# Turning the expert mask on VectorE in 32-column blocks, in an audio tower kernel of one core

## The chip, the cores and the metric

The kernel runs on one core of one Trainium2 chip. The metric is device time in microseconds (us) of one execution, from several executions; the profile comes from one further execution, whose own time is given beside its span.

Engines are named as in the profile: PE is TensorE's matmul stream, PEld its weight loads (LDWEIGHTS), DVE is VectorE, ACT is ScalarE, POOL is GpSimd, SP is SyncE, whose queue issues the DMAs here.

## What is computed

```python
# x: [16, 375, 256] float32; row 0 of each batch entry is the readout row
h = gelu(x[:, 1:] @ W_other + x[:, :1] @ W_read + b)     # [16, 374, 256]
h = h + cosine_attention(layernorm(h))                   # softmax of cosines, + its input
h = h + moe_attention(layernorm(h))
# moe_attention, per token t and expert e (8 experts, D = 128):
logits = (x/|x|) @ (sim/|sim|) - sigmoid(gates)
mask   = (relu(logits) > 0), or the two largest where no expert is active
r      = softmax over the active experts of relu(logits)
q, k, v = sum_e mask[t, e] * (x[t] @ W_{q,k,v}[e])       # each [T, 128]
a      = softmax(causal(q k^T / sqrt(128))) v
out    = sum_e mask*r[t, e] * (a[t] @ W_o[e])
```

So for every batch entry a 0/1 mask of 374 tokens by 8 experts is worked out, and the normalised rows x are multiplied by it, once for every expert, before the q, k and v products.

## The kernel before, in words

Tokens lie in NT = 3 tiles of 128 (TP = 384, the last tile holds 118), channels in NC = 2 chunks of 128, E = 8. Every float32 product is made as three fp16 products of high and low parts (split_product, from L1616; its three matmuls carry L1620). The 16 batch entries run through a software pipeline. One step works on up to four entries at once: `g1` (first layer norm), `f` (cosine attention, second layer norm, router, mask), `m` (the q, k, v products, called "units" M(0) to M(23), six matmuls each) and `n` (scores, softmax, and the output products, called "pairs" 0 to 11, three matmuls of 512 columns each). The pipeline (from L325) has an early step, one step with fixed indices, a hardware loop of 12 steps, one more full step with fixed indices, and two shorter ones. The 12 + 2 full steps have both an `f` and an `n`. Ahead of the pipeline a head embeds all entries and takes the first ones through their first stages.

Each engine has its order of work written out by hand, and engines meet only through semaphores. What matters around the change, in a full step:

- PE (its `step`, second half) runs M(12), logits(f), pair 2, M(13), M(14), pair 3, M(15), turn_mask(f), pair 4, M(16), pair 5 and so on. logits gives the router's products. turn_mask (L1701 to L1706) transposes the three tiles of mask16, each 128x128 of which 8 columns are used, into a PSUM bank. pair(n, p) waits until DVE has added pair p-2 (s_pair_added), since two PSUM banks alternate: pair 4 needs the additions of pairs 0, 1 and 2.
- DVE runs pairs(0, 2), route(f), pairs(2, 4), weight_max, head_low of k, pairs(4, 5) and so on. route (L1168 to L1213) is the chain of small operations that goes from the router's products to the mask; nearly all of them wait for the one before. Its last two write the mask, once as mask16 in fp16 (L1211) and once as lg[8] in float32 (L1212) for POOL. add_pair (L1130 to L1137) is the addition of one pair from PSUM to h.
- ACT copies the turned mask to maskT, 8x384 (turned_mask, L798 to L802), between the scaling of pairs 3 and 4, and then evacuates k (head_high).
- SP, in mask_around (L423 to L433), waits for maskT, stores it to DRAM in one DMA (8 rows of 768 B), waits for that, and loads it back, spread over 128 partitions, in two DMAs of half the experts each. mask_tokens (from L1215) on DVE multiplies x by it, one expert at a time; the first one is called after pair 8 has been added.

Of the kernel before, what the change touches and what calls it, by code (L numbers as in the profile page):

```python
# [26 lines left out]
def audio_tower_kernel(nc, x, tok_w, tok_b, sim_matrix, gates, q_proj, k_proj, v_proj, o_proj, out):  # L27
# [6 lines left out]
    NC = C // P  # L34
    PAIRS = NT * E // 2

    KEYS = [min((i + 1) * P, T) for i in range(NT)]
# [7 lines left out]
    with ExitStack() as ctx:  # L45
# [3 lines left out]
        def sem(name):  # L49
            return ctx.enter_context(nc.semaphore(name))  # L50
# [50 lines left out]
        row3 = sb("row3", [P, 6, NT])  # L101
        mask16 = sb("mask16", [P, NT, P], F16)
        maskT = sb("maskT", [E, TP], F16)
        mask_all = sb("mask_all", [P, E, TP], F16)
        route_w = sb("route_w", [P, B, NT, E])
        xm = sb("xm", [P, E, 2 * NC, TP], F16)
# [53 lines left out]
        d_route = nc.dram_tensor("d_route", [(NT - 1) * E * P], F32, kind="Internal").ap()  # L160
        d_mask = nc.dram_tensor("d_mask", [B, E * TP], F16, kind="Internal").ap()

# [95 lines left out]
        s_route_exp = sem("route_exp")  # L258
        s_mask_turned = sem("mask_turned")
        s_mask_row = sem("mask_row")  # L260
# [114 lines left out]
        def _(sp):  # L375
# [47 lines left out]
            def mask_around(f):  # L423

                sp.wait_ge(s_mask_row, f + 1).then_inc(s_sp_passed, 1)
                sp.dma_start(d_mask[f, :].rearrange("(e t) -> e t", e=E), maskT[:, :]).then_inc(s_mask_stored, 16)
                sp.wait_ge(s_mask_stored, 16 * (f + 1)).then_inc(s_sp_passed, 1)
                if later(f):
                    sp.wait_ge(s_xm_ready, E * f).then_inc(s_sp_passed, 1)
                for k in range(2):  # L430
                    sp.dma_start(mask_all[:, k * (E // 2):(k + 1) * (E // 2), :].rearrange("p e t -> p (e t)"),
                                 d_mask[f, k * (E // 2) * TP:(k + 1) * (E // 2) * TP].partition_broadcast(P)).then_inc(
                                     s_mask_loaded[k], 16)  # L433
# [266 lines left out]
        def _(act):  # L700
# [8 lines left out]
            act.wait_ge(s_pad_zeroed, 1)  # L709
            a.activation(unused[:, :], mask16[:, 0, 0:1], ACT.Gelu)  # L710

# [85 lines left out]

            def turned_mask(f):  # L798
                act.wait_ge(s_mask_turned, f + 1)
                if later(f):  # L800
                    act.wait_ge(s_mask_stored, 16 * f)
                a.activation(maskT[:, :], as16(turn[1] if later(f) else turn[0], TP)[0:E, :], ACT.Copy).then_inc(s_mask_row, 1)  # L802

            def route_exp(f):
# [47 lines left out]
            def step(i, g1, f, m, n):  # L852
# [20 lines left out]
                if early(m):  # L873
                    weights_high(2 * NC - 1)
                    turned_rows_2(f)
                    weights_high(2 * NC)
                    weights_high(2 * NC + 1)
                    head_high(qT, qkv_bank[0], s_q_done, m + 1, s_q_hi, [], qkv_out)
                    turned_mask(f)
                    route_exp(f)  # L880
                    head_high(kT, qkv_bank[1], s_k_done, m + 1, s_k_hi, [], qkv_out)
                    high(0, g1)
                    output_weights_high(0)
                    output_weights_high(1)
                    turned_rows(g1)
                    high_v()
                    return
# [28 lines left out]
                if f is not None and n is not None:  # L916
                    scale_pairs(0, 4)
                    turned_mask(f)
                    head_high(kT, qkv_bank[1], s_k_done, m + 1, s_k_hi, [(s_scores_done, NT * m)], qkv_out)
                    scale_pairs(4, 5)  # L920
                    route_exp(f)
                    scale_pairs(5, 7)
                    if g1 is not None:
                        high(0, g1)
                    scale_pairs(7, PAIRS)
                    if g1 is not None:
                        turned_rows(g1)
                    high_v()
                    return
# [66 lines left out]
            exp_cosines(1, (2,))  # L996
            turned_mask(0)
            route_exp(0)
# [10 lines left out]
        def _(dve):  # L1009
            v = nc.vector  # L1010


            v.memset(mask16[:, 0, :], 0.0).then_inc(s_pad_zeroed, 1)
            v.memset(h[96:P, 0:1, NT - 1, :], 0.0).then_inc(s_zeroed, 1)
# [5 lines left out]
            v.memset(read_hl[:, :], 0.0).then_inc(s_zeroed, 1)  # L1020
            v.memset(mask16[:, 1:NT, :], 0.0)

# [145 lines left out]
            def route(b):  # L1168
# [20 lines left out]
                if later(b):  # L1189
# [17 lines left out]
                                             row3[:, 1, :].unsqueeze(2).broadcast_to([P, NT, E]),  # L1207
                                             ALU.is_lt, ALU.mult))
                if later(b):
                    dve.wait_ge(s_mask_turned, b)  # L1210
                v.tensor_tensor(mask16[:, :, 0:E], lg[:, 0, :, :], M, ALU.add).then_inc(s_mask_ready, 1)  # L1211
                v.tensor_tensor(lg[:, 8, :, :], lg[:, 0, :, :], M, ALU.add).then_inc(s_mask_ready, 1)  # L1212
                assert at[0] == RP  # L1213
# [302 lines left out]
        def _(pe):  # L1516
# [43 lines left out]
            for k in range(WARM):  # L1560
                t_.matmul(bank[6][:, 0:P], mask16[:, 0, :], mask16[:, 0, :], start=True, stop=True)  # L1561
            pe.wait_ge(s_consts, 1)
# [6 lines left out]
            for k in range(FILL):  # L1569
                t_.matmul(bank[6][:, 0:P], mask16[:, 0, :], mask16[:, 0, :], start=True, stop=True)  # L1570
            pe.wait_ge(s_tok_read, 16)
# [26 lines left out]
            def turn_first_high(b):  # L1598

                pe.wait_ge(s_hi1, b + 1)  # L1600
                if not isinstance(b, int) or b > 1:
                    pe.wait_ge(s_logits_out, b)
                    pe.wait_ge(s_mask_row, b)
                turn_rows(0, b, 0, turn[0], s_turned1_hi)
# [83 lines left out]
            def logits(f):  # L1688
# [10 lines left out]
                last.then_inc(s_logits_done, 1)  # L1699

            def turn_mask(f):  # L1701
                pe.wait_ge(s_mask_ready, 2 * (f + 1))
                pe.wait_ge(s_T2_lo, f + 1)
                for t in range(NT):
                    last = t_.transpose(as16(turn[1] if later(f) else turn[0], TP)[:, t * P:(t + 1) * P], mask16[:, t, :], ident16[:, :])  # L1705
                last.then_inc(s_mask_turned, 1)  # L1706

# [95 lines left out]
            def step(i, g1, f, m, n):  # L1803
# [19 lines left out]
                if early(m):  # L1823
# [5 lines left out]
                    M(*range(7, 13))  # L1829
                    turn_mask(f)  # L1830
                    M(*range(13, 22))
# [6 lines left out]
                if f is not None and n is not None:  # L1838
# [37 lines left out]
                    M(15)  # L1876
                    turn_mask(f)
                    pair(n, 4)
# [13 lines left out]
                pe.wait_ge(s_logits_out, B)  # L1892
                pe.wait_ge(s_mask_row, B)
                turn_v(n)
# [74 lines left out]
            turn_in(13)  # L1969
            turn_mask(0)  # L1970
            dots(1, 2)
# [9 lines left out]
            pe.wait_ge(s_hi2, 2)  # L1981
            pe.wait_ge(s_mask_row, 1)
            turn_rows(1, 1, 0, turn[0], s_turned2_hi)
# [26 lines left out]
```

## Time and profile before

| | |
|---|---|
| median of 3 runs | 712.61 us (712.33 to 713.15) |
| the profiled execution's own time | 712.67 us |
| its span, first to last instruction | 710.9 us |
| granted TensorE clock | 1.00 of full speed |
| busy: PE / PEld | 705.6 us (99%) / 472.8 us (66%) |
| busy: DVE / ACT / POOL | 579.4 us (81%) / 378.8 us (53%) / 400.5 us (56%) |
| one loop step | 40.50 us |

In a row of a timeline the columns are start in us from the span's start, duration in us, engine, line, operation, output and input tiles with shapes, the count of instructions merged into the row, and in brackets the idle time before it and what ended it. PE matmuls are pipelined and overlap, so that the start of the next group, not the duration of this one, tells what a group cost. A line inside a helper stands for all its callers; the tile names tell them apart: `xm,w_qkv` are the units M, `w_o,aoT` the pairs, `ident,mask` the turned mask.

### The profile page before, as it was taken

To read this page: it belongs to the slowest core of one execution; us is meant where nothing else is said; L and a number is where in the kernel's file an instruction comes from. 1 tells how busy PE (TensorE), PEld (TensorE's weight loads), DVE (VectorE), ACT (ScalarE), POOL (GpSimd) and SP (SyncE) were. 2 spreads that over 40 slices of the span, in tenths; PEclk is the share of its full clock that TensorE was granted. 3 is DMA by queue.
4 is the path that set the end of the run, shared out by engine and by line. 5 is a ranking of instruction groups with operands and counts; after the bars stand their busy time and mean duration, and the time that the engine had idled before them with its cause. 6 is when DMAs were issued, how large, how long until landed. Compare 5 with 4: busy or idle time off the path is not lost.

```text
span 710.9 us, 18143 instructions
## 1 busy us (share of the span) xinstructions
PE 705.6 (99%) x5416; PEld 472.8 (66%) x5416; DVE 579.4 (81%) x1453; ACT 378.8 (53%) x808; POOL 400.5 (56%) x655
## 2 busy tenths in 40 slices
PE   9999999999999999999999999999999999999997
PEld 8888666675757666575756666575766667575655
DVE  5788798888879888888979888887988888886636
ACT  4977373554646464563646355463646455464443
POOL 7652325757465566746566575746566674643434
DMA  9671210202020010202020010202011020201120
GB/s 246 159 179 46 75 43 13 67 3 65 12 63 14 25 52 0 70 7 63 14 56 22 12 66 0 70 7 63 14 34 43 0 70 7 63 17 53 16 74 30
DMA packets 33430, 34.35 MB, mean 48 GB/s; under 512 B 7288, under 2 KB 29176, under 8 KB 33272
## 3 DMA queue, kind: packets, MB, share of 16 engines
q1 hardware_dynamic: 33152, 33.78, 17.7%
q8 instruction: 16, 0.26, 0.2%
q10 hardware_dynamic: 248, 0.19, 0.1%
q14 instruction: 14, 0.11, 0.1%
HBM read 27.70 MB, written 6.26 MB: 48 GB/s over the span
## 4 chain that ended last, share of the span: by engine, by line
PE 98%; DVE 1%; ACT 0%; issue 0%; DVEq 0%
PE bank L1620 76%; PE bank L1683 7%; PE bank L1537 4%; PE bank L1594 3%; PE bank L1526 2%; PE bank L1754 1%; PE bank L1669 1%; PE bank L1542 1%; PE bank L1732 1%; PE bank L1561 1%; PE bank L1705 0%; PE bank L1694 0%; PE bank L1697 0%; ACT xm L836 0%; PE bank L1795 0%
## 5 line engine op out<-in xcount | busy, mean ns | idle before, releaser
L1620 PE MATMUL bank<-xm,w_qkv 128*128 128x374 f16 x2304 | 415.7, 322 | 0.0
L1620 PEld LDWEIGHTS bank<-xm,w_qkv 128*128 128x128 f16 x2304 | 220.8, 98 | 139.2
L866 ACT ACTIVATE region_c<-bank,out_w 128x256 f32<-128x256 f32 x180 | 84.6, 470 | 163.5 <-PE bank L1620 162.5
L1224 DVE TENSOR_TENSOR xm<-xT,mask_all 128x1496 f16<-128x1496 f16 x128 | 151.8, 1208 | 0.0
L1620 PE MATMUL bank<-w_o,aoT 128*128 128x512 f16 x540 | 143.3, 379 | 0.0
L1136 DVE SCALAR_TENSOR_TENSOR h<-bank,out_w,h 128x256 f32 (+1 forms) x180 | 86.5, 480 | 49.1 <-ACT region_c L866 44.3
L645 POOL TENSOR_TENSOR region_c<-region_c 128x512 f32<-128x512 f32 x46 | 76.4, 1661 | 27.8 <-ACT region_c L866 23.1
L660 POOL TENSOR_TENSOR exp_hl<-exp,exp_hl 128x128 f16<-128x128 f32 (+2 forms) x48 | 41.9, 873 | 83.8 <-ACT exp_hl L822 83.3
L1620 PEld LDWEIGHTS bank<-w_o,aoT 128*128 128x128 f16 x540 | 50.5, 98 | 39.6
L1115 DVE TENSOR_SCALAR region_b<-h,moments,small 128x256 f32 (+1 forms) x96 | 48.8, 552 | 6.1 <-POOL small L566 6.1
L648 POOL TENSOR_TENSOR region_c<-region_c 128x256 f32<-128x256 f32 x46 | 47.9, 1041 | 8.2 <-POOL region_c L645 8.2
L1683 PE MATMUL bank<-xhl,exp_hl 128*128 128x257 f16 (+1 forms) x432 | 50.3, 272 | 0.0
L651 POOL TENSOR_TENSOR h<-region_c,h 128x256 f32 (+1 forms) x46 | 38.0, 827 | 15.8 <-POOL region_c L648 11.4
L1683 PEld LDWEIGHTS bank<-xhl,exp_hl 128*128 128x128 f16 x432 | 41.6, 97 | 7.3
L745 ACT ACTIVATE xhl<-region_b 128x768 f16<-128x768 f32 x32 | 27.0, 844 | 33.1 <-DVE region_b L1115 33.1
L775 ACT ACTIVATE region_a<-region_a,log_p,small 128x374 f32<-128x374 f32 (+2 forms) x48 | 28.2, 587 | 26.4 <-DVE region_a L1235 26.4
L562 POOL TENSOR_SCALAR small<-moments 128x3 f32<-128x3 f32 x32 | 14.4, 449 | 49.4 <-DVE moments L1107 49.4
L1620 PE MATMUL bank<-xT 128*128 128x374 f16 (+2 forms) x288 | 37.8, 268 | 0.0
L1537 PE MATMUL bank<-w_tok,xinT 128*128 128x256 f16 x288 | 37.6, 273 | 0.0
L850 ACT ACTIVATE pT<-bank 128x768 f16<-128x768 f16 x16 | 13.0, 810 | 46.0 <-PE bank L1754 46.0
L1098 DVE BATCH_NORM_STATS2 stats<-h 128x6 f32 (+1 forms) x96 | 35.7, 413 | 0.0
L576 POOL TENSOR_TENSOR small<-small,m_half 128x3 f32<-128x3 f32 x32 | 28.3, 884 | 8.1 <-POOL small L572 8.1
(198 smaller groups left out, 1064.4 us busy)
## 6 DMA issues: line engine op xcount, KB each, us to landing
mask_all<-d_mask SPq DMA_DIRECT2D x32, 384.0 KB, 3.8
h<-in_x_dram SPq DMA_DIRECT2D x16, 256.0 KB, 4.9
out_dram<-h SPq DMA_DIRECT2D x32, 128.0 KB
rnorm_row<-d_rnorm SPq DMA_DIRECT2D x16, 192.0 KB, 3.8
out_dram<-h SPq DMA_DIRECT2D x16, 112.0 KB
h<-in_x_dram SPq DMA_DIRECT2D x15, 112.0 KB, 5.2
xm<-in_L_ffn_q_proj_dram SPq DMA_DIRECT2D x2, 512.0 KB, 7.6
region_c<-in_L_ffn_k_proj_dram SPq DMA_DIRECT2D x2, 512.0 KB, 6.2
```

Source lines behind the costliest of these rows:

```text
L645: g.tensor_tensor(prod_sum[:, 0:2, :], prod[:, buf, 0:2, :], prod[:, buf, 2:4, :], ALU.add).then_inc(s_tile_summed, 1)
L648: g.tensor_tensor(prod_sum[:, 2, :], prod_sum[:, 0, :], prod_sum[:, 1, :], ALU.add).then_inc(s_tile_summed, 1)
L651: g.tensor_tensor(h[:, n, t, :], prod_sum[:, 2, :], h[:, n, t, :], ALU.add).then_inc(s_tile_ready, 1)
L660: done = g.tensor_tensor(exp2_hl[:, 1, sl], exp2[:, sl], exp2_hl[:, 0, sl], ALU.subtract)
L866: a.activation(prod[:, prod_buf(n, t), q, :], pair_bank(n, p)[:, C:2 * C], ACT.Copy, scale=weights_out(n)[:, t, 2 * q + 1:2 * q + 2]).then ...
L1098: v.bn_stats(stats[n][:, t, :], h[:, b, t, :]).then_inc((s_stats1, s_stats2)[n], 1)
L1115: v.tensor_scalar(xs[n][:, t, :], h[:, b, t, :], moments[n][:, t, 0:1], small[n][:, 4, t:t + 1], ALU.subtract, ALU.mult).then_inc((s_xs1, ...
L1136: v.scalar_tensor_tensor(h[:, n, t, :], pair_bank(n, p)[:, 0:C], weights_out(n)[:, t, e0:e0 + 1], h[:, n, t, :], ALU.mult, ALU.add).then_i ...
L1224: v.tensor_tensor(xm[:, e, :, 0:T], xT[1][:, :, :, 0:T].rearrange("p a c t -> p (a c) t"), mask_all[:, e, 0:T].unsqueeze(1).broadcast_to([ ...
L1537: t_.matmul(projected(t), xinT[:, b % 2, xp, c, t * P:(t + 1) * P], w_tok[:, wp, c, :], start=(c == 0 and xp == 0 and wp == 0), stop=False ...
L1620: last = t_.matmul(dst, left[lp], right[rp], start=(starts and k == 0), stop=(stops and k == 2), skip_group_check=True)
L1683: last = t_.matmul(banks[t][:, 0:n], exp1_hl[:, ep, j, t * P:(t + 1) * P], xhl[0][:, xp, j, 0:n], start=(j == 0 and k == 0), stop=(j == NT ...
```

## The change

DVE turns the mask itself. mask16 shrinks to 32 columns, with column e*3 + t for expert e and token tile t (24 used). After the two mask operations of route, DVE waits for the first of them, waits for the stores of the previous entry's mask, and transposes the 128x32 tile in four 32x32 blocks into mask_turned: row q*32 + e*3 + t holds the mask of tokens 32q to 32q+31 of tile t. SP stores the four blocks in four DMAs of 24 rows of 64 B, such that DRAM holds what it held before (expert, then token), and loads it back as before. PE's three transposes, their two waits, the waits of PE and DVE for their result and ACT's copy are gone. The block of zeros that warms PE up is now a part of mask_all.

```diff
+    SQ = 32
...
-        mask16 = sb("mask16", [P, NT, P], F16)
-        maskT = sb("maskT", [E, TP], F16)
+        mask16 = sb("mask16", [P, SQ], F16)
+        mask_turned = sb("mask_turned", [P, SQ], F16)
...
                 sp.wait_ge(s_mask_row, f + 1).then_inc(s_sp_passed, 1)
-                sp.dma_start(d_mask[f, :].rearrange("(e t) -> e t", e=E), maskT[:, :]).then_inc(s_mask_stored, 16)
-                sp.wait_ge(s_mask_stored, 16 * (f + 1)).then_inc(s_sp_passed, 1)
+                rows = d_mask[f, :].rearrange("(r b j) -> b r j", r=SQ, j=SQ)
+                for q in range(P // SQ):
+                    sp.dma_start(rows[q][0:NT * E, :], mask_turned[q * SQ:q * SQ + NT * E, :]).then_inc(s_mask_stored, 16)
+                sp.wait_ge(s_mask_stored, 16 * (P // SQ) * (f + 1)).then_inc(s_sp_passed, 1)
...
-            def turned_mask(f):
-                act.wait_ge(s_mask_turned, f + 1)
-                if later(f):
-                    act.wait_ge(s_mask_stored, 16 * f)
-                a.activation(maskT[:, :], as16(turn[1] if later(f) else turn[0], TP)[0:E, :], ACT.Copy).then_inc(s_mask_row, 1)
...
                 if later(b):
-                    dve.wait_ge(s_mask_turned, b)
-                v.tensor_tensor(mask16[:, :, 0:E], lg[:, 0, :, :], M, ALU.add).then_inc(s_mask_ready, 1)
-                v.tensor_tensor(lg[:, 8, :, :], lg[:, 0, :, :], M, ALU.add).then_inc(s_mask_ready, 1)
+                v.tensor_tensor(mask16[:, 0:NT * E].rearrange("p (e t) -> p t e", t=NT), lg[:, 0, :, :], M,
+                                ALU.add).then_inc(s_mask_ready, 1)
+                v.tensor_tensor(lg[:, 8, :, :], lg[:, 0, :, :], M, ALU.add).then_inc(s_mask_ready, 1)
+                dve.wait_ge(s_mask_ready, 2 * b + 1)
+                if later(b):
+                    dve.wait_ge(s_mask_stored, 16 * (P // SQ) * b)
+                v.transpose(mask_turned[:, :], mask16[:, :]).then_inc(s_mask_row, 1)
...
-            def turn_mask(f):
-                pe.wait_ge(s_mask_ready, 2 * (f + 1))
-                pe.wait_ge(s_T2_lo, f + 1)
-                for t in range(NT):
-                    last = t_.transpose(as16(turn[1] if later(f) else turn[0], TP)[:, t * P:(t + 1) * P], mask16[:, t, :], ident16[:, :])
-                last.then_inc(s_mask_turned, 1)
```

All calls of turned_mask and turn_mask go too, and PE's waits for s_mask_row in front of later uses of the banks.

## Rows read from the trace of the kernel before

**Rows 1.** The page: busy time and share of the span by engine.
```profile
PE 705.6 (99%) x5416; PEld 472.8 (66%) x5416; DVE 579.4 (81%) x1453; ACT 378.8 (53%) x808; POOL 400.5 (56%) x655
```
**Rows 2.** Busy time by engine in one loop step: start:end, step length, busy us (instructions).
```profile
297.00:337.50 40.50, 40.50 (x310) 26.32 (x308) 34.46 (x88) 21.21 (x47) 24.71 (x40) 1.00 0.12 34
```
**Rows 3.** Waits of PE over the whole span: who for whom, us, times, longest.
```profile
PE bank L1561 <- DVE mask L1013: 1.1, 1, 1.1
PE bank L1620 <- DVE v_tok L1310: 0.4, 1, 0.4
PE bank L1795 <- ACT xm L836: 0.4, 1, 0.4
```
**Rows 4.** Timeline of PE in a loop step, from the router's products to pair 4.
```profile
320.89 0.19 PE L1697 MATMUL bank<-w_sim,xT 128*128 128x8 f16 x2
320.94 0.81 PE L1620 MATMUL bank<-w_o,aoT 128*128 128x512 f16 x3
...
324.13 1.11 PE L1620 MATMUL bank<-xm,w_qkv 128*128 128x374 f16 x6
325.08 0.33 PE L1705 MATMUL bank<-ident,mask 128*128 128x128 f16 x3
325.25 0.38 PE L1620 MATMUL bank<-w_o,aoT 128*128 128x512 f16 x1
```
**Rows 5.** Timeline of PE's weight loads around the turned mask, same step.
```profile
325.08 0.15 PEld L1705 LDWEIGHTS bank<-ident,mask 128*128 128x128 f16 x2
325.19 0.10 PEld L1620 LDWEIGHTS bank<-w_o,aoT 128*128 128x128 f16 x1
```
**Rows 6.** Timeline of DVE in the same step: route and the additions around it.
```profile
321.12 0.21 DVE L1182 COPY logit_parts<-bank 128x48 f32<-128x48 f32 x1
321.36 0.18 DVE L1185 TENSOR_TENSOR lg<-logit_parts 128x24 f32<-128x24 f32 x1
321.57 0.18 DVE L1187 TENSOR_TENSOR lg<-lg,small 128x24 f32<-128x24 f32 x1
321.89 0.18 DVE L1191 TENSOR_TENSOR lg<-lg,sig 128x24 f32<-128x24 f32 x1
...
322.54 0.35 DVE L1196 TENSOR_TENSOR cmp<-lg 128x192 f32<-128x192 f32 x1
322.93 0.18 DVE L1197 TENSOR_REDUCE row<-lg 128x3 f32<-128x24 f32 x1
...
324.47 0.18 DVE L1211 TENSOR_TENSOR mask<-lg 128x24 f16<-128x24 f32 x1
324.57 0.17 DVE L1212 TENSOR_TENSOR lg<-lg 128x24 f32<-128x24 f32 x1
```
**Rows 7.** Timeline of DVE, the addition of pair 2 alone, same step.
```profile
324.67 0.47 DVE L1136 SCALAR_TENSOR_TENSOR h<-bank,out_w,h 128x256 f32 x1
```
**Rows 8.** The same two places in the full step ahead of the loop.
```profile
122.07 1.06 DVE L1136 SCALAR_TENSOR_TENSOR h<-bank,out_w,h 128x256 f32<-128x256 f32 x2
...
122.69 0.10 PEld L1620 LDWEIGHTS bank<-w_o,aoT 128*128 128x128 f16 x1
```
**Rows 9.** Timeline of PEld and PE in the head, where PE waited for DVE.
```profile
58.75 0.11 PEld L1669 LDWEIGHTS bank<-ident,exp_hl 128*128 128x128 f16 x2 [0.24 <-DVE exp_hl L1245]
...
58.76 0.34 PE L1669 MATMUL bank<-ident,exp_hl 128*128 128x128 f16 x3
```
**Rows 10.** Timeline of PE in the head and the early step, around the turned mask.
```profile
55.74 0.33 PE L1705 MATMUL bank<-ident,mask 128*128 128x128 f16 x3
56.02 0.48 PE L1620 MATMUL bank<-xT 128*128 128x118 f16 x6
...
84.41 0.33 PE L1705 MATMUL bank<-ident,mask 128*128 128x128 f16 x3
84.58 0.64 PE L1620 MATMUL bank<-xm,w_qkv 128*128 128x374 f16 x3
```
**Rows 11.** Timeline of ACT, the copy of the turned mask, same loop step.
```profile
325.53 0.48 ACT L802 ACTIVATE maskT<-bank 8x384 f16<-8x384 f16 x1 [0.73 <-PE bank L1705]
325.92 0.45 ACT L751 ACTIVATE kT<-bank 128x374 f16<-128x374 f32 x1
```
**Rows 12.** Timeline of SP's queue in the same step: norms, mask store, mask loads.
```profile
323.79 0.37 SPq L421 DMA_DIRECT2D rnorm_row<-d_rnorm  x1
326.25 0.30 SPq L426 DMA_DIRECT2D d_mask<-maskT  x1
327.93 0.90 SPq L431 DMA_DIRECT2D mask_all<-d_mask  x2
```
**Rows 13.** Timeline of DVE, the first use of the mask in the same step.
```profile
333.58 1.02 DVE L1224 TENSOR_TENSOR xm<-xT,mask_all 128x1496 f16<-128x1496 f16 x1
```
**Rows 14.** DMA issues by line: transfers, count, KB each, median us to landing.
```profile
mask_all<-d_mask SPq DMA_DIRECT2D x32, 384.0 KB, 3.8
...
d_rnorm<-small SPq DMA_DIRECT2D x16, 1.5 KB, 2.4
...
d_route<-route_w SPq DMA_DIRECT2D x1, 8.0 KB, 10.7
```

More of the change, by code:

```diff
@@ L101, in audio_tower_kernel @@
         row3 = sb("row3", [P, 6, NT])
-        mask16 = sb("mask16", [P, NT, P], F16)
-        maskT = sb("maskT", [E, TP], F16)
+        mask16 = sb("mask16", [P, SQ], F16)
+        mask_turned = sb("mask_turned", [P, SQ], F16)
         mask_all = sb("mask_all", [P, E, TP], F16)
+        zeros16 = mask_all[:, 0, 0:P]
         route_w = sb("route_w", [P, B, NT, E])
@@ L160, in audio_tower_kernel @@
         d_route = nc.dram_tensor("d_route", [(NT - 1) * E * P], F32, kind="Internal").ap()
-        d_mask = nc.dram_tensor("d_mask", [B, E * TP], F16, kind="Internal").ap()
+        d_mask = nc.dram_tensor("d_mask", [B, SQ * P], F16, kind="Internal").ap()
         bank = [ctx.enter_context(nc.psum_tensor(f"bank{i}", [P, 512], F32)) for i in range(8)]
@@ L258, in audio_tower_kernel @@
         s_route_exp = sem("route_exp")
-        s_mask_turned = sem("mask_turned")
         s_mask_row = sem("mask_row")
@@ L709, in _ @@
             act.wait_ge(s_pad_zeroed, 1)
-            a.activation(unused[:, :], mask16[:, 0, 0:1], ACT.Gelu)
+            a.activation(unused[:, :], zeros16[:, 0:1], ACT.Gelu)
             def split_in(b):
@@ L878, in step @@
                     head_high(qT, qkv_bank[0], s_q_done, m + 1, s_q_hi, [], qkv_out)
-                    turned_mask(f)
                     route_exp(f)
@@ L917, in step @@
                     scale_pairs(0, 4)
-                    turned_mask(f)
                     head_high(kT, qkv_bank[1], s_k_done, m + 1, s_k_hi, [(s_scores_done, NT * m)], qkv_out)
@@ L996, in _ @@
             exp_cosines(1, (2,))
-            turned_mask(0)
             route_exp(0)
@@ L1010, in _ @@
             v = nc.vector
-            v.memset(mask16[:, 0, :], 0.0).then_inc(s_pad_zeroed, 1)
+            v.memset(zeros16, 0.0).then_inc(s_pad_zeroed, 1)
             v.memset(h[96:P, 0:1, NT - 1, :], 0.0).then_inc(s_zeroed, 1)
@@ L1020, in _ @@
             v.memset(read_hl[:, :], 0.0).then_inc(s_zeroed, 1)
-            v.memset(mask16[:, 1:NT, :], 0.0)
+            v.memset(mask16[:, :], 0.0)
             def token_weights_low():
@@ L1560, in _ @@
             for k in range(WARM):
-                t_.matmul(bank[6][:, 0:P], mask16[:, 0, :], mask16[:, 0, :], start=True, stop=True)
+                t_.matmul(bank[6][:, 0:P], zeros16, zeros16, start=True, stop=True)
             pe.wait_ge(s_consts, 1)
@@ L1569, in _ @@
             for k in range(FILL):
-                t_.matmul(bank[6][:, 0:P], mask16[:, 0, :], mask16[:, 0, :], start=True, stop=True)
+                t_.matmul(bank[6][:, 0:P], zeros16, zeros16, start=True, stop=True)
             pe.wait_ge(s_tok_read, 16)
@@ L1602, in turn_first_high @@
                     pe.wait_ge(s_logits_out, b)
-                    pe.wait_ge(s_mask_row, b)
                 turn_rows(0, b, 0, turn[0], s_turned1_hi)
@@ L1829, in step @@
                     M(*range(7, 13))
-                    turn_mask(f)
                     M(*range(13, 22))
@@ L1876, in step @@
                     M(15)
-                    turn_mask(f)
                     pair(n, 4)
@@ L1892, in step @@
                 pe.wait_ge(s_logits_out, B)
-                pe.wait_ge(s_mask_row, B)
                 turn_v(n)
@@ L1969, in _ @@
             turn_in(13)
-            turn_mask(0)
             dots(1, 2)
@@ L1981, in _ @@
             pe.wait_ge(s_hi2, 2)
-            pe.wait_ge(s_mask_row, 1)
             turn_rows(1, 1, 0, turn[0], s_turned2_hi)
```

## The prediction

> **What bounds the kernel now.** I read the page first: PE is busy 99% of the span, DVE 81% [rows 1]. Then the stretch of one loop step: PE is busy for all of its 40.50 us, DVE for 34.46 [rows 2], and over the whole span PE's waits in the trace add up to 1.9 us [rows 3]. So PE sets the end, and whatever leaves its stream shortens the time, unless something that PE has just not had to wait for comes late instead. A list of waits does not show that second thing: a release that comes in the very last moment leaves no idle time. So the next view is the timeline at the place of the edit, engine by engine.
>
> On PE the three transposes of the mask start at 325.08 and pair 4 starts at 325.25 [rows 4]: they cost 0.17 us. Pair 4's first weight load, which carries pair 4's wait for the addition of pair 2, starts at 325.19 [rows 5]. On DVE that addition stands right behind route; it starts at 324.67 and takes 0.47 us, so it ends at 325.14 [rows 7], 0.05 us before the load that waits for it. Pair 4 is thus at the edge of two chains that both start at the router's products: PE's own (pair 2, M(13), M(14), pair 3, M(15), the transposes) and DVE's (route, whose first copy starts at 321.12, then the addition) [rows 4, 6, 7]. The transposes are the cover under which DVE arrives in time. In the full step ahead of the loop the margin is a little wider: 122.07 + 0.47 = 122.54 against a load at 122.69, 0.15 us [rows 8].
>
> **PE: three transposes removed.** Taken alone 0.17 us a time, 16 times, 2.7 us. In the head it is worth nothing: behind the transposes PE next starts at 56.02 [rows 10], where three transposes at 0.055 us each would have let it start at 55.90, so it waits there for something else. In the early step the next unit starts right behind them, 84.41 to 84.58 [rows 10], with no pair behind it: 0.17 us gained. In the 14 full steps the next instruction is pair 4, and there DVE decides.
>
> **DVE: one transpose and two waits added, between the mask and the addition of pair 2.** Queued behind them are the additions of pairs 2 and 3, weight_max and the low half of k; PE waits for the first of these. Call x the delay of that addition. DVE's rows give what such steps cost, start to start: 0.10 us where the next operation waits for nothing (324.47 to 324.57), 0.21 where it waits for the result just made (321.36 to 321.57), 0.32 where it does so and a second, old semaphore with a value computed from the loop index stands beside it (321.57 to 321.89, L1190) [rows 6]. The last is the form of the new code: the transpose waits for mask16 just written at L1211 and for the old stores with a computed value. The operation on lg[8] lies in the shadow of that wait. So I place the transpose at 324.47 + 0.32 = 324.79.
>
> No row shows a DVE transpose. From below it is a small operation like L1211 that lets the next one start 0.10 us on. From above it is like a 192-element operation which holds the next one for 0.39 (322.54 to 322.93) [rows 6]: it reads 32 elements a partition, far nearer to the 24 of L1211. For the central value I take 0.20, that is 0.10 for the slot and as much again because the addition behind it brings a wait and a computed value of its own, which before lay in the shadow of L1211 and L1212 and now comes behind a stalled queue. The addition then starts at 324.99 instead of 324.67: x = 0.32. The lower bound is 324.47 + 0.21 + 0.10 - 324.67 = 0.11 (second wait and its arithmetic free), the upper 324.47 + 0.32 + 0.39 - 324.67 = 0.51. A gain is excluded here: nothing leaves DVE's chain but a wait for the previous entry's transposes, which is a step old. The strided output of L1211 has as many elements as before; I take it as nothing.
>
> How late is PE then? When PE really waits, its matmul follows the load within 0.01 us (58.75, 58.76) [rows 9]; now it is 0.06 us behind it, 325.19 to 325.25 [rows 4, 5]. So pair 4 can start about 0.05 us closer behind the addition than it does, and a loop step changes by x - 0.05: 0.27 us longer. The 0.17 us that the transposes leave is already in this: the place they leave is filled by waiting. In the two full steps outside the loop (no values to compute, so x about 0.21, margin 0.15) it is 0.06 us longer. Nothing later on PE can win it back, since its stream has no idle time in which to do so [rows 2].
>
> **ACT: the copy removed.** 0.48 us at 325.53, and k is evacuated right behind it [rows 11]. ACT is idle before it and PE's next need of k is a step away: worth nothing, but k comes some tenths earlier, and that is the slack in which the delayed additions of pair 3 and 4 fit.
>
> **SP: four stores in place of one.** Queued behind them are only the loads of the mask and, later, stores of the result; the norms have gone out at 323.79 [rows 12]. The store now starts at 326.25 and the loads at 327.93, 1.68 later. After, SP is released by DVE at about 324.79 + 0.2 = 325.0 and issues at about 325.2. Two issues with their index arithmetic take 0.90, of which one is about 0.37, so each further one is 0.53: the fourth goes out at 326.8. With 1.68 for its way the loads go out at 328.5, and with the 2.4 that a store of 128 short rows takes (d_rnorm) at 329.2 [rows 12, 14]. The first load lands 3.8 us later, at 332.3 to 333.0, and DVE asks for it at 333.58 [rows 13, 14]. Hidden; without that cover DVE's additions of pairs 9 to 11 would wait for it.
>
> As to the short rows: here 1.5 KB in short rows take 2.4 us and 8 KB in single values 10.7 us [rows 14]. The Trainium skill ("DMA: Bandwidth & Descriptors", Specifications) says that line rate needs transfers of at least 512 B and that below it the DMA engine reads, modifies and writes; the rows now stored have 64 B instead of 768 B. By that rule the stores get slower, but for 6 KB the rows above leave it inside the cover.
>
> **The sum**, on the profiled execution's 712.67 us (span 710.9, 1.8 us around it; it lies 0.06 above the median): 12 x 0.27 = 3.2; 2 x 0.06 = 0.1; early step -0.17; head, ACT and SP 0. Together +3.1, so 715.8 us.
>
> **Rivals.**
> First, faster: PE's stream alone decides. It would be so if DVE's additions were hidden, x at most 0.05 (or, to gain anything, below it), the point from which the sign turns. Then 15 x 0.17 = 2.5 us go and the time is 710.1. For it speaks the 99% of PE [rows 1]; against it, that pair 4's load starts 0.05 us behind the addition in this step and that even the cheapest row makes x 0.11. A whole gain needs x below -0.12 in the loop.
>
> Second, the waits cost nothing and only a slot of 0.10 to 0.11 us is added: 12 x (0.11 - 0.05) = 0.7, 2 x (0.11 - 0.15) = -0.1, early -0.17: +0.4, 713.1 us, which a measurement of this kernel can hardly tell from no change (that limit is 0.2%, 1.4 us; 711.2 to 714.0). For it: the two waits are for things that are done or nearly so. Against it: 0.21 and 0.32 between dependent operations [rows 6]. The Trainium skill ("VectorE: DVE Perf Modes", "The DRAIN you can't avoid") says that the next operation starts only when the pipe is empty and that a semaphore costs nothing extra, so that one should count operations, not waits. The rows differ on both: the next operation starts 0.10 us into one of 0.18, and the dependent one 0.21 behind. By that rule one more operation of 0.18 would be all: x = 0.18, +1.6 us from the loop and about 714.1.
>
> Third, the stores land late. It decides from the point where the last of them takes over about 1.7 + 1.3 us. At d_route's 10.7 us the loads would go out at 337.5 and land at 341.3, DVE would be held for 7.7 us at 333.58, and 14 steps would cost up to 14 x 7.7 = 108 us, 820 us. Against it: d_route writes 2,048 single values, these stores 96 rows in all.
>
> **How the numbers follow.** Forecast (x from 0.17 to 0.51): 0.74. Second rival, no change to be told: 0.16. First rival: 0.07. Third: 0.03. The range reaches from the lower bound's 713.0 to the upper bound's: 12 x 0.46 = 5.5, 2 x 0.36 = 0.7, -0.17, together +6.0, 718.7. Slower by over 0.2%: 0.74 + 0.03 = 0.77; within: 0.16; faster: 0.07.
>
> **What would show it.** In a loop step after: the transpose at about 0.32 us behind the mask operation; the addition of pair 2 about 0.5 behind it instead of 0.20; between M(15) and pair 4 a hole on PE of about 0.4 us that is put down to DVE's addition (L1136), where the transposes stood; a step of 40.77 us instead of 40.50; the mask's loads landed before DVE asks. The prediction is wrong if pair 4 follows M(15) without a hole (then x or my reading of the margin), if the step is longer but the hole is elsewhere, or if DVE waits for the mask.

## The result, and the profile after

The changed kernel takes 716.16 us (median of 6 runs, 715.89 to 716.35); the kernel before, run beside it, 712.87 (712.33 to 713.23). The ratio is 1.0049, 95% interval 1.0039 to 1.0059: 3.3 us slower. The profiled execution took 716.35 us with a span of 714.6; before it was 712.67 and 710.9.

The page after, busy time by engine (before: [rows 1]):

```profile
PE 705.5 (99%) x5368; PEld 469.2 (66%) x5368; DVE 580.8 (81%) x1469; ACT 374.6 (52%) x792; POOL 400.5 (56%) x655
```

It says almost nothing. PE has 48 matmuls fewer, DVE 16 instructions more, and every share is the same to a per cent. The waits of PE, over the whole span, are the view that has changed (before: [rows 3]):

```profile
PE bank L1616 <- DVE h L1130: 3.5, 12, 0.3
PE bank L1558 <- DVE mask_all L1007: 1.1, 1, 1.1
PE bank L1616 <- DVE v_tok L1307: 0.4, 1, 0.4
PE bank L1784 <- ACT xm L833: 0.3, 1, 0.3
```

L1130 is the addition of a pair (L1136 before). Twelve waits, one in each step of the hardware loop, together 3.5 us: that is the loss. The loop step by itself (start:end, length, busy us of PE, PEld, DVE, ACT and POOL, with instructions; before: [rows 2]):

```profile
297.00:337.80 40.80, 40.51 (x305) 26.10 (x304) 34.59 (x89) 20.95 (x45) 24.71 (x40) 1.00 0.11 34
```

And the place, on PE (before: [rows 4]):

```profile
322.18 0.19 PE L1693 MATMUL bank<-w_sim,xT 128*128 128x8 f16 x2
322.23 0.81 PE L1616 MATMUL bank<-w_o,aoT 128*128 128x512 f16 x3
...
325.42 1.11 PE L1616 MATMUL bank<-xm,w_qkv 128*128 128x374 f16 x6
326.82 0.39 PE L1616 MATMUL bank<-w_o,aoT 128*128 128x512 f16 x1 [0.29 <-DVE h L1130]
```

and on DVE (before: [rows 6, 7]):

```profile
325.77 0.20 DVE L1203 TENSOR_TENSOR mask<-lg 128x24 f16<-128x24 f32 x1
325.87 0.18 DVE L1205 TENSOR_TENSOR lg<-lg 128x24 f32<-128x24 f32 x1
326.10 0.21 DVE L1209 STREAM_TRANSPOSE mask_turned<-mask 128x32 f16<-128x32 f16 x1
326.28 1.07 DVE L1130 SCALAR_TENSOR_TENSOR h<-bank,out_w,h 128x256 f32 x2
```

M(15) starts at 325.42 and six matmuls of 0.158 us later, at 326.37, pair 4 could start. It starts at 326.82, 0.45 us later. The transposes took 0.17 of this before; the other 0.28 is new, and within 0.02 us it is what the step has grown. On DVE the transpose comes 0.33 us behind the mask operation and the addition of pair 2 0.51 behind it, against 0.20 before.

Where the 3.64 us between the last matmuls of the two traces arose, by the first of the router's products in each step (head 47.08 and 47.17, early step 78.41 and 78.66, first full step 118.14 and 118.21, loop 158.63 and 158.72, last full step 644.63 and 648.26): +0.25 in and ahead of the head (0.09 up to its first product, 0.16 behind it), -0.18 in the early step, +0.02 in the first full step, 12 x 0.295 = 3.54 in the loop, +0.01 behind it.

### The profile page after: what moved, and what is told of

It reads as the page before. It is cut to its first block, busy times and chain, and to the rows that moved or that the text cites. A ratio compares the mean times of both kernels' runs of the same rounds, so it can differ in the third digit from the quotient of the medians.

```text
span 714.6 us, 18146 instructions
## 1 busy us (share of the span) xinstructions
PE 705.5 (99%) x5368; PEld 469.2 (66%) x5368; DVE 580.8 (81%) x1469; ACT 374.6 (52%) x792; POOL 400.5 (56%) x655
## 4 chain that ended last, share of the span: by engine, by line
PE 89%; DVE 8%; issue 1%; ACT 0%; POOL 0%; DVEq 0%; POOLq 0%
PE bank L1616 69%; PE bank L1679 7%; PE bank L1534 4%; PE bank L1591 3%; PE bank L1523 1%; PE bank L1743 1%; DVE h L1130 1%; PE bank L1665 1%; PE bank L1721 1%; PE bank L1558 1%; DVE lg L1197 1%; DVE cmp L1196 1%; DVE cmp L1192 1%; PE bank L1539 1%; DVE cmp L1190 1%
## 5 line engine op out<-in xcount | busy, mean ns | idle before, releaser
L1221 DVE TENSOR_TENSOR xm<-xT,mask_all 128x1496 f16<-128x1496 f16 x128 | 149.6, 1192 | 0.0
L1130 DVE SCALAR_TENSOR_TENSOR h<-bank,out_w,h 128x256 f32 (+1 forms) x180 | 86.7, 482 | 57.6 <-ACT region_c L863 53.7
```

The costliest lines, as they stand in the source:

```text
L1130: v.scalar_tensor_tensor(h[:, n, t, :], pair_bank(n, p)[:, 0:C], weights_out(n)[:, t, e0:e0 + 1], h[:, n, t, :], ALU.mult, ALU.add).then_i ...
L1221: v.tensor_tensor(xm[:, e, :, 0:T], xT[1][:, :, :, 0:T].rearrange("p a c t -> p (a c) t"), mask_all[:, e, 0:T].unsqueeze(1).broadcast_to([ ...
```

## The experiments

All runs are compared with the kernel before, run on the same chip beside them (712.65, 712.92 and 712.71 us in the three sets).

**The transpose behind the addition of pair 2.** The changed kernel, with one move; turn_mask stands for the two waits and the transpose, which leave route:

```diff
                     pairs(0, 2)
                     route(f)
-                    pairs(2, 4)
+                    pairs(2, 3)
+                    turn_mask(f)
+                    pairs(3, 4)
```

> The changed kernel with one edit: on VectorE the transpose and its two waits stand behind the addition of pair 2, not ahead of it. Theory (pair 4 on TensorE waits for that addition, and the 0.31 us that the transpose puts ahead of it is the whole loss): the addition starts 0.20 us behind the mask operation as before the change, so pair 4 starts where it did before, with a hole of about 0.14 us left where the transposes stood; a loop step takes 40.48 us instead of 40.80 and the time is 716.2 - 12 x 0.32 = 712.4. Rival (the four small stores or their way through DRAM hold the step up): the mask leaves VectorE 0.4 us later, so the time is 716.2 or more. Rival (more work on VectorE anywhere costs): no change, 716.2.

Measured: 711.92 us, ratio 0.9989 (0.9980 to 0.9998), a loop step of 40.46. The same instructions in another order on one engine are 4.2 us faster (4.0 if each kernel is set against the kernel before beside it). PE around pair 4:

```profile
323.47 1.11 PE L1623 MATMUL bank<-xm,w_qkv 128*128 128x374 f16 x6
324.54 0.82 PE L1623 MATMUL bank<-w_o,aoT 128*128 128x512 f16 x3
```

Pair 4 could start at 323.47 + 0.95 = 324.42 and starts at 324.54. A hole of 0.12 us is left: DVE is still the later of the two, as it had been all along under the cover of the transposes.

**The kernel before, with the VectorE transpose added.** Everything of the old way is kept; this is put behind the operation on lg[8], with its result unused:

```diff
+                dve.wait_ge(s_mask_ready, 2 * b + 1)
+                if later(b):
+                    dve.wait_ge(s_mask_stored, 16 * b)
+                v.transpose(mask_turned[:, :], mask16[:, 0, 0:32])
```

> The kernel before, with TensorE's transposes, ScalarE's copy and the one store all kept, and the VectorE transpose with its two waits added, its result not used. Theory: the addition of pair 2 is 0.31 us later as in the changed kernel, TensorE's transposes lie in the time in which it would wait, a loop step takes 40.80 us as in the changed kernel; the early step keeps its 0.17: 716.3 us. Rival (the two costs add): 40.97 a step, 718.2. Rival (the loss comes from the stores or from DRAM, not from VectorE): 712.9.

Measured: 715.89 us, ratio 1.0047 (1.0033 to 1.0060), 40.77 a step. PE:

```profile
325.00 1.11 PE L1625 MATMUL bank<-xm,w_qkv 128*128 128x374 f16 x6
325.95 0.33 PE L1710 MATMUL bank<-ident,mask 128*128 128x128 f16 x3
326.38 0.82 PE L1625 MATMUL bank<-w_o,aoT 128*128 128x512 f16 x3
```

With PE's transposes kept, a step takes what it takes without them, since they lie in the time in which PE waits. The loss comes from the two waits and the transpose on DVE alone, and the removal of PE's transposes gave nothing in the loop.

**Without the wait for the old stores.**

```diff
                 dve.wait_ge(s_mask_ready, 2 * b + 1)
-                if later(b):
-                    dve.wait_ge(s_mask_stored, 16 * (P // SQ) * b)
                 v.transpose(mask_turned[:, :], mask16[:, :]).then_inc(s_mask_row, 1)
```

> The changed kernel without VectorE's wait for the stores of the entry before (they are over, since VectorE has since used the mask that was loaded from them). In the loop that wait brings an instruction that computes its value. Theory (each such instruction of VectorE's queue costs 0.10 us behind a dependent wait): the transpose starts 0.22 us behind the mask operation instead of 0.33, x is 0.21 instead of 0.31, a loop step takes 40.70 us, the time is 716.2 - 12 x 0.10 = 715.0. Rival (waits are free, only the operation costs): 716.2.

Measured: 714.96 us, ratio 1.0029 (1.0017 to 1.0040), 40.68 a step. DVE:

```profile
325.02 0.20 DVE L1203 TENSOR_TENSOR mask<-lg 128x24 f16<-128x24 f32 x1
325.12 0.18 DVE L1205 TENSOR_TENSOR lg<-lg 128x24 f32<-128x24 f32 x1
325.25 0.21 DVE L1207 STREAM_TRANSPOSE mask_turned<-mask 128x32 f16<-128x32 f16 x1
325.42 1.07 DVE L1130 SCALAR_TENSOR_TENSOR h<-bank,out_w,h 128x256 f32 x2
```

A wait on a semaphore that has long reached its value costs 0.10 us here, 0.33 to 0.23 between mask operation and transpose. It is not the waiting that costs, but the instruction that computes the value out of the loop index: in the full step ahead of the loop, where the value is fixed, the changed kernel has the same wait, and its transpose stands 0.23 us behind the mask operation too (0.24 there without the wait).

```profile
121.96 0.20 DVE L1203 TENSOR_TENSOR mask<-lg 128x24 f16<-128x24 f32 x1
...
122.19 0.21 DVE L1209 STREAM_TRANSPOSE mask_turned<-mask 128x32 f16<-128x32 f16 x1
122.33 1.03 DVE L1130 SCALAR_TENSOR_TENSOR h<-bank,out_w,h 128x256 f32<-128x256 f32 x2
```

For the loop the rival of free waits falls.

**A copy in place of the transpose.**

```diff
-                v.transpose(mask_turned[:, :], mask16[:, :]).then_inc(s_mask_row, 1)
+                v.tensor_copy(mask_turned[:, :], mask16[:, :]).then_inc(s_mask_row, 1)
```

> The changed kernel with a plain copy of the same 128x32 tile where the transpose stands, all waits kept; the experts then get a mask that is not turned, so that the data of the q, k and v products are others while all sizes and orders stay. Theory (a slot and two waits, whatever the operation): 716.2 and 40.80 a step. Rival (the transpose itself holds VectorE longer than a copy): the addition of pair 2 comes up to 0.1 us sooner behind it, 40.70 a step, 715.0.

Measured: 716.12 us, 40.79 a step. DVE:

```profile
325.62 0.18 DVE L1209 COPY mask_turned<-mask 128x32 f16<-128x32 f16 x1
325.80 1.07 DVE L1130 SCALAR_TENSOR_TENSOR h<-bank,out_w,h 128x256 f32 x2
```

The transpose takes 0.21 us and the copy 0.18, and in the loop both let the addition start 0.18 behind them. So in the loop it plays no part that it is a transpose. In the full step ahead of the loop, where the addition's own wait has no value to compute, the two differ: the addition starts 0.14 behind the transpose (122.19, 122.33 above) and 0.09 behind the copy:

```profile
121.79 0.17 DVE L1209 COPY mask_turned<-mask 128x32 f16<-128x32 f16 x1
121.88 1.07 DVE L1130 SCALAR_TENSOR_TENSOR h<-bank,out_w,h 128x256 f32<-128x256 f32 x2
```

**One store in place of four.**

```diff
-                for q in range(P // SQ):
-                    sp.dma_start(rows[q][0:NT * E, :], mask_turned[q * SQ:q * SQ + NT * E, :]).then_inc(s_mask_stored, 16)
+                sp.dma_start(d_mask[f, :].rearrange("(p j) -> p j", j=SQ), mask_turned[:, :]).then_inc(s_mask_stored, 16)
```

> The changed kernel with one store of all 128 rows of 64 B in place of four of 24 rows; the mask then lies in DRAM in another order, so that the experts get other tokens' masks, while all sizes and the rest of the order stay. Theory (the stores are hidden): the loads go out some 1.5 us sooner and nothing else moves, 716.2 and 40.80 a step. Rival (the four stores cost): under 715.

Measured: 716.28 us, 40.79 a step. SP's queue in the changed kernel, where four stores were issued (before: [rows 12]):

```profile
326.24 0.37 SPq L422 DMA_DIRECT2D rnorm_row<-d_rnorm  x1
326.87 1.83 SPq L429 DMA_DIRECT2D d_mask<-mask_turned  x4
330.23 0.95 SPq L434 DMA_DIRECT2D mask_all<-d_mask  x2
```

and with one:

```profile
326.14 0.34 SPq L427 DMA_DIRECT2D d_mask<-mask_turned  x1
329.15 0.90 SPq L432 DMA_DIRECT2D mask_all<-d_mask  x2
```

From the first store to the loads it is 3.36 us with four stores and 3.01 with one, against 1.68 for the one store of long rows in [rows 12]; the medians of all 16 stores are 3.59, 3.00 and 1.73. One would put most of this down to the short rows, but the rows around it say otherwise. In the last full step no load of norms goes out ahead, and the one store of 128 short rows takes 1.60 us:

```profile
652.14 0.37 SPq L427 DMA_DIRECT2D d_mask<-mask_turned  x1
653.74 0.84 SPq L432 DMA_DIRECT2D mask_all<-d_mask  x2
```

There the kernel before takes 1.42 and the changed one 2.63. In the other 13 full steps SP issues a load of the norms (192 KB) 0.6 to 2.5 us ahead of the mask's store, and with short rows the loads of the mask always go out at the same distance behind the landing of that load: 0.3 to 0.5 us with one store and 0.9 to 1.0 with four. With the long rows it is 0.1 to 0.3 in 10 steps of 13. So by these traces most of the time between store and loads is the landing of the norms' load. The short rows themselves cost 0.2 us where no such load is ahead, and about 0.6 in steps where the store goes out 0.63 behind it in each kernel (2.41 with long rows, 2.89 and 3.08 with short ones); that there are four costs 0.5 to 1.0. No run moved the norms' load to try this. Either way the stores are hidden: no step changed.

**The addition of pair 2 inside route.** To give the change what it was made for, the addition must not stand behind route at all. ACT has scaled pair 2 long before; a gap is behind the is_equal comparison, where between() is now the addition of pair 2:

```diff
-                after(v.tensor_tensor(square[1], others, mine, ALU.is_equal))
+                v.tensor_tensor(square[1], others, mine, ALU.is_equal).then_inc(s_route_dve, 1)
+                at[0] += 1
+                if between is not None:
+                    between()
+                dve.wait_ge(s_route_dve, RP * b + at[0])
```

> The changed kernel with one edit: the addition of pair 2 stands inside route, in the gap behind the is_equal comparison, so it ends some 1.2 us before TensorE asks for it. Theory: no hole between M(15) and pair 4, a loop step takes 40.50 - 0.17 = 40.33 us, and the time is 716.2 - 12 x 0.47 - 2 x 0.19 = 710.2, under both kernels. The mask comes about 0.35 us later, which its loads can bear. Rival (the stores or the mask's way decide): 716.2 or more. Rival (the next thing on VectorE, the addition of pair 3, takes the place of pair 2's): between 710.2 and 716.2, with the hole ahead of pair 5.

Measured: 712.61 us, ratio 0.9997 (0.9988 to 1.0006), 40.52 a step. The forecast missed by 2.4 us. PE shows that pair 4 does follow M(15) at once, 0.95 us behind it, and that another hole has opened in the next step:

```profile
324.69 1.11 PE L1620 MATMUL bank<-xm,w_qkv 128*128 128x374 f16 x6
325.64 0.81 PE L1620 MATMUL bank<-w_o,aoT 128*128 128x512 f16 x3
...
345.28 1.11 PE L1620 MATMUL bank<-xm,w_qkv 128*128 128x374 f16 x6
346.37 0.51 PE L1669 MATMUL bank<-ident,exp_hl 128*128 128x128 f16 x6
```

345.28 + 0.95 = 346.23, and the transposes of exp start at 346.37, 0.14 us late.

**The same move in the kernel before,** with turn_mask on PE put behind pair 4.

> The kernel before with the same move of the addition of pair 2 into route, and TensorE's three transposes of the mask behind pair 4 instead of ahead of it, so that they don't wait for the later mask. It separates the move from the change. Theory: the kernel before had no idle time on TensorE, so the move gives nothing: a loop step of 40.50 us and 712.9 us, within 0.1%. Rival (the gain expected of the changed kernel with this move is the move's own): 710.2 here too.

Measured: 720.68 us, ratio 1.0113 (1.0098 to 1.0129), 41.14 a step. Both theories missed this, by 8 and by 10 us, and it showed what the last run had only hinted at. PE's largest wait was for exp:

```profile
PE bank L1673 <- DVE exp_hl L1249: 5.2, 12, 0.5
```

Followed back from there, DVE has its mask products (xm<-xT,mask_all) in front of it. POOL in this kernel:

```profile
331.25 0.31 POOL L636 TENSOR_TENSOR lg<-lg,row 128x24 f32<-128x24 f32 x1 [1.59 <-DVE row L1299]
...
332.41 1.27 POOL L645 TENSOR_TENSOR region_c<-region_c 128x512 f32<-128x512 f32 x1 [0.34 <-POOL route_w L638]
...
335.63 1.61 POOL L613 TENSOR_TENSOR xhl<-region_b,xhl 128x768 f16<-128x768 f32 x1
337.20 1.97 POOL L645 TENSOR_TENSOR region_c<-region_c 128x512 f32<-128x512 f32 x1
```

and DVE's mask products in the same stretch:

```profile
336.35 1.68 DVE L1228 TENSOR_TENSOR xm<-xT,mask_all 128x1496 f16<-128x1496 f16 x1
...
338.35 1.61 DVE L1228 TENSOR_TENSOR xm<-xT,mask_all 128x1496 f16<-128x1496 f16 x1
```

The first product starts while POOL is in L613, which ends at 335.63 + 1.61 = 337.24, and it ends at 338.03, 0.79 behind that. The second starts inside L645, which ends at 339.17, and ends at 339.96, again 0.79 behind. In the kernel before, the first product takes 1.02 us [rows 13]; it starts at 333.58 and POOL's L613 ends at 333.81, 0.79 ahead of its end. So in these places the product ends 0.79 us after POOL's operation does, whenever it was started. The Trainium skill ("SBUF — State Buffer", Terms, shared port pair) says that VectorE and GpSimd share one pair of ports, held for a whole instruction, and that the loser blocks. The trace agrees: of the 0.93 us that such a product takes without a POOL operation (shown below), 0.79 are still to come when POOL ends.

That makes a third chain beside those of the prediction: mask, POOL's route_weights (which waits for ACT and DVE in its middle), its additions of the pairs, DVE's mask products behind them, exp, PE's transposes of exp. From the router's products to the first of POOL's long additions it is 8.35 us in the kernel before, 8.30 in the last run and 9.00 here, and the loop step here is 0.64 longer than 40.50. Why it is longer here stands in ACT's order:

```profile
328.95 0.48 ACT L802 ACTIVATE maskT<-bank 8x384 f16<-8x384 f16 x1 [1.37 <-PE bank L1709]
```

PE's transposes now come behind the three matmuls of pair 4, so that ACT copies the turned mask 5.54 us behind the router's first product (323.41), against 4.90 before (325.53 in [rows 11], first product at 320.63). Behind that copy ACT evacuates k, DVE's low half of k waits for k, and behind it on DVE stand the operations of weight_max for which POOL waits at L636; each of these is 0.64 later than before. So by the trace it is the second half of this edit, the transposes put behind pair 4, that cost the 8 us, and not the addition moved into route; neither half was run alone. In the run with pair 2 inside route this chain kept its length while PE's stream between its two ends had lost 0.17 us: nearly all of that came back as the hole of 0.14.

**GpSimd's wait filled.** add_tile(n, 0), POOL's three operations on the pairs 0 to 3, is put into the middle of route_weights; all the rest is the kernel with pair 2 inside route:

```diff
                                       row3[:, 2, :].unsqueeze(2).broadcast_to([P, NT, E]), ALU.subtract))
+                if between is not None:
+                    between()
                 pool.wait_ge(s_weigh_dve, 3 * b + 3).then_inc(s_pool_passed, 1)
```

> The kernel with pair 2 inside route (712.6, 40.52 a step, its hole of 0.14 us ahead of the transposes of exp), and on GpSimd the three operations of add_tile(n, 0) moved into the middle of route_weights, where GpSimd waits about 1 us for ScalarE and VectorE. Theory (the hole comes from GpSimd's chain, whose long additions hold VectorE's mask products back until they are over): that chain ends up to 0.5 us sooner, the hole closes, nothing but TensorE's own stream is left, a loop step takes 40.33 us, and the time is 712.6 - 12 x 0.19 = 710.3. Rival (the hole comes from something else on VectorE): 40.52 and 712.6 again.

Measured: 710.33 us, ratio 0.9965 (0.9951 to 0.9979). The windows of a loop step:

```profile
297.00:337.33 40.33, 40.33 (x305) 26.17 (x304) 34.05 (x89) 21.14 (x47) 23.45 (x40) 1.00 0.13 34
```

PE is busy for the whole of 40.33 us, 0.17 less than before the change. A mask product of DVE that meets no long POOL operation:

```profile
341.37 0.93 DVE L1227 TENSOR_TENSOR xm<-xT,mask_all 128x1496 f16<-128x1496 f16 x1
```

And the same two moves in the kernel before:

> The same two moves in the kernel before (its transposes on TensorE kept, behind pair 4). Theory (720.7 without the move on GpSimd came from GpSimd's chain, which started 0.65 us late): the chain is no longer in the way, TensorE's own stream decides, a loop step takes 40.50 us and the time is 712.9; beside the run with the changed kernel this gives what the change is worth where nothing else is at its edge, 12 x 0.17 + 2 x 0.17 + 0.17 = 2.5 us. Rival (TensorE's transposes and ScalarE's copy, now later, still hold pair 6 or the k products): above 714.

Measured: 712.68 us, ratio 1.0000 (0.9990 to 1.0009), 40.50 a step. The two moves bring the old kernel nothing (the late copy of ACT does no harm here), and with both of them in place the change is worth 712.68 - 710.33 = 2.35 us. Three transposes 15 times come to 2.5, and the head takes 0.15 of it back (see below).

**Another order without the move into route.** The float32 mask first, then pair 2, then mask16 and its transpose (without the wait for the old stores), then pair 3.

> The changed kernel in another order on VectorE: the float32 mask for GpSimd first, then the addition of pair 2, then mask16 and its transpose (without the wait for the old stores), then the addition of pair 3. Theory: the addition of pair 2 and GpSimd's chain both start 0.10 us sooner than in the kernel with the transpose behind pair 2 (711.9, a step of 40.46); the hole ahead of pair 4 falls from 0.12 to 0.02 us, a loop step takes 40.36 us, and the time is 711.9 - 12 x 0.10 = 710.7. What could take it back: the mask is stored 0.3 to 0.4 us later, of about 1.0 us that its loads have. Rival (the chain over GpSimd to the transposes of exp on TensorE, which held the kernel with pair 2 inside route, is the next bound): between 710.7 and 712, with a hole ahead of those transposes.

Measured: 711.13 us, ratio 0.9977 (0.9968 to 0.9986), 40.44 a step where 40.36 was expected. DVE:

```profile
323.90 0.18 DVE L1204 TENSOR_TENSOR lg<-lg 128x24 f32<-128x24 f32 x1
324.07 0.48 DVE L1131 SCALAR_TENSOR_TENSOR h<-bank,out_w,h 128x256 f32 x1
```

The addition starts 0.17 us behind the small operation, not 0.10 as in [rows 6, 7] (324.57, 324.67): there a second small operation had covered the addition's own wait and computed value. So 0.03 us came of the 0.10 looked for, and the hole ahead of pair 4 was still 0.10. Of the 0.8 us between this run and the one with the transpose behind pair 2, the loop gives only 12 x 0.02 = 0.2; 0.3 comes in the head.

## Why the prediction was right

**The bound and the margin.** Right: PE's stream sets the end, and pair 4 stood at the edge of a second chain on DVE. The run with the added transpose shows both at once.

**x.** Predicted 0.32 from the rows of dependent operations and the queue's own instructions; measured 0.31 (0.51 - 0.20). The parts agree too: 0.33 to the transpose against 0.32, 0.18 behind it against 0.20. The run without the old wait confirms the first part, and the one with the copy the second. The rule of the Trainium skill that was weighed there (semaphores free, x = 0.18, 714.1 us) is not borne out in the loop: one more operation of 0.18 would have left a step at about 40.63. In the full step with fixed indices it does come out: x is 0.37 - 0.19 = 0.18. What it leaves out here is the 0.13 us more for values computed from the loop index.

**A loop step.** Predicted 0.27 longer, measured 0.295. The term that was too large is the 0.05 us by which pair 4 could start closer behind the addition: the addition ends at 326.28 + 0.47 = 326.75 and pair 4 starts 0.07 behind, against 0.11 before, and x in the traces' own figures is 0.31, so the margin was 0.02 to 0.04. 12 x 0.025 = 0.3 us of the sum.

**The full steps outside the loop.** Predicted 0.06 each, measured 0.02 and 0.01, since x is 0.18 there and not 0.21.

**The early step.** Predicted -0.17, measured -0.18.

**The head.** Predicted 0, measured +0.25. Of this 0.09 was there before the router's first product, and it belongs to the execution: that product starts anywhere from 46.7 to 47.8 us in the traces of all the runs. The other 0.16 is the step that failed. I saw that PE waits behind the transposes [rows 10] and took it that their removal brings nothing; I didn't ask for whom PE waits. It is DVE's cosines (the operation that reads rnorm_row), and the transpose stands ahead of them. DVE and PE after:

```profile
55.47 1.70 DVE L1232 SCALAR_TENSOR_TENSOR region_a<-rnorm_row,small,bank 128x384 f32<-128x384 f32 x3
...
56.26 0.48 PE L1616 MATMUL bank<-xT 128*128 128x118 f16 x6
```

The cosines started at 55.22 before and PE at 56.02: both are about 0.25 later, start included. The runs show whose work it is. From the router's products in the head to those in the early step it is 31.33 us in the kernel before, 31.33 and 31.31 in its two variants without a transpose on DVE, 31.45 in the one with that transpose added, and 31.49 in the changed kernel. So the transpose and its wait make 0.12 of the 0.16. In the variants of the changed kernel it is 31.45 to 31.47, and 31.17 only where the float32 mask comes first.

**ACT.** As predicted, nothing, while PE turned the mask ahead of pair 4. Where it did so 0.65 us later, ACT's copy was on the chain that set the step (41.14 us).

**SP.** Right that it is hidden. Its parts were off: the first store goes out 4.64 us behind pair 2's start (326.87 - 322.23) where 4.26 was reckoned, since in this step SP still issues the load of the norms at 326.24 (4.3 in the steps after it). From the first store to the loads it is 3.36 us, near the 3.3 reckoned (325.2 to 328.5); but the 1.68 taken from the kernel before for a store's way was for the most part the landing of the norms' load, which the prediction had down as gone out and of no further account. The first load of the mask lands 3.6 us after its issue, at 333.8, and DVE's first mask product starts at 335.17: a cover of 1.3 us, and no wait of DVE for the mask is in the trace. The rule of the Trainium skill on transfers under 512 B was weighed there for its direction. That is borne out by a small amount, 1.60 us against 1.42 in the last full step with one store each; whether reading before writing is the reason, no run here shows.

**Together.** 3.1 predicted, 3.3 measured between the medians, 3.68 between the profiled executions. The small errors of loop and head add up to 0.5, and the profiled execution lay at the upper end of its runs.

**The rivals.** The first (PE alone decides, 710.1 us) did not happen in the changed kernel, but its price was right: with the two other chains out of the way the kernel takes 710.33. I had named one chain at the edge; there were two, and the second, over POOL, takes back nearly all of that gain by itself (712.61). The second rival (only a slot, x = 0.11) falls with the measured 0.31, the third with the 3.36 to 3.98 us of the stores in the loop.

## What to carry to other kernels

A kernel whose first engine is busy for all of a step can have other chains that arrive within hundredths of a microsecond, and no list of waits shows them: before work is taken off the first engine, look for each instruction just behind it at when its release came. Where an operation goes from the bound engine to another one, its place in that engine's order can decide more than its cost: here the same instructions gave 716.2 and 711.9 us in two orders, and 710.3 with the addition inside route and another engine's order changed too. Put the moved work behind whatever the bound engine waits for next.

## What the hardware showed unexpectedly

- A DVE product of 128x1496 fp16 takes 0.93 us where POOL is not in a long operation, and else ended 0.79 us after that operation's end: 1.02, 1.68 and 1.61 us in the places shown. POOL's order is thus a part of DVE's time.
- A wait that is long fulfilled costs 0.10 us of DVE's queue in a hardware loop, where its value is computed from the loop index, if nothing ahead of it on the engine covers it. With a fixed value the same wait cost nothing (0.23 us from mask operation to transpose with it, 0.24 without).
- A 32x32 block transpose of 128x32 fp16 on DVE takes 0.21 us, a copy of the same tile 0.18. The next operation, with its own wait, starts 0.18 us behind either in the loop; with fixed values it starts 0.14 behind the transpose and 0.09 behind the copy.
- In the last full step 128 rows of 64 B to DRAM took 1.60 us from issue until the next DMA behind it was issued, four stores of 24 such rows 2.63, and 8 rows of 768 B 1.42. With a load of 192 KB issued 0.6 to 1.6 us ahead on the same queue the first two took 2.7 to 3.3 and 3.4 to 4.0: the next DMA went out 0.3 to 0.5 and 0.9 to 1.0 us after that load had landed.
